# Rope and nope rows of an attention group loaded whole, after the group before it in the same place

## The reference, cut to what matters

```
q  = (ql @ Wqu)  -> 16 heads x 16 features      ("nope" part of the query)
qr = rope(ql @ Wqr) -> 16 heads x 64 features   (rotary part of the query)
k  = (ckv @ Wku) -> 16 heads x 16 features      (nope part of the key)
kr = rope(x @ Wkr)  -> 64 features, one for all heads
scores = (q k^T + qr kr^T) / sqrt(80), causal mask, softmax over s
out = softmax(scores) v
```

## Time and profile before

| | |
|---|---|
| median of 3 runs | 1025.59 us (1021.88 to 1035.82) |
| the profiled execution | 1023.33 us, span 1021.5 us |
| TensorE (PE) busy | 881.4 us, 86% of the span |
| VectorE (DVE) busy | 565.9 us, 55% |
| ScalarE (ACT) busy | 381.5 us, 37% |
| GpSimd (POOL) busy | 228.1 us, 22% |
| mean granted TensorE clock | 0.901 of full |
| bytes moved by DMA | 69.96 MB, 68 GB/s over the span |

### The profile page before, as it was taken

One profiled execution on the slowest core, in us unless ns is written; L12 is line 12 of the kernel. 1 busy time (PEld: TensorE's weight loads), 2 busy tenths in 40 slices (PEclk: granted clock), 3 DMA queues, 4 the chain that ended last, 5 costly groups with the idle time before them and its releaser, 6 DMA issues.

```text
span 1021.5 us, 11944 instructions
## 1 busy us (share of the span) xinstructions
PE 881.4 (86%) x4799; PEld 509.0 (50%) x4799; DVE 565.9 (55%) x988; ACT 381.5 (37%) x470; POOL 228.1 (22%) x209
## 2 busy tenths in 40 slices
PE   3988598999899986898698998978999879969897
PEld 3443244344335432453346878543333248868676
DVE  4697264767476544651533355377777335954452
ACT  2312043444444433446334340213555664410331
POOL 2451032233112303411310100220111126710010
PEclk9987598899799967999787999876999989989799
DMA  5389416521922292001300000494400042000001
GB/s 169 83 214 176 115 42 132 96 63 50 175 46 51 82 172 84 2 14 57 137 9 1 1 0 19 143 173 69 58 2 1 1 185 73 1 1 1 1 1 42
DMA packets 37936, 69.96 MB, mean 68 GB/s; under 512 B 6085, under 2 KB 14829, under 8 KB 37877
## 3 DMA queue, kind: packets, MB, share of 16 engines
q1 hardware_dynamic: 37880, 69.20, 29.1%
HBM read 49.07 MB, written 18.38 MB: 66 GB/s over the span
## 4 chain that ended last, share of the span: by engine, by line
PE 59%; DVE 17%; DMA 9%; ACT 5%; SPq 5%; POOL 3%; issue 2%; DVEq 0%; ACTq 0%; POOLq 0%
PE psD L1572 10%; PE psO L1693 9%; PE psA L1572 9%; PE psD L1638 8%; DVE mx L1180 7%; PE psO L1572 7%; PE psA L1656 7%; SPq L471 5%; PE psA L1655 3%; DVE hid_low L1486 2%; PE psD L1640 2%; DMA d_gq<-Pr 1%; PE psA L1604 1%; DMA Qs<-mrowb 1%; ACT Pr L908 1%
## 5 line engine op out<-in xcount | busy, mean ns | idle before, releaser
L1180 DVE TENSOR_REDUCE mx<-psD 128x1 f32<-128x512 f32 (+3 forms) x417 | 260.9, 658 | 143.1 <-PE psD L1640 101.9
L908 ACT ACTIVATE Pr<-psA 128x1024 f32<-128x1024 f32 (+3 forms) x192 | 162.3, 865 | 226.2 <-PE psA L1656 225.5
L779 POOL TENSOR_SCALAR_AFFINE_SELECT Pr<-Pr 128x512 f32<-128x512 f32 x96 | 60.9, 635 | 432.9 <-ACT Pr L908 360.6
L1655 PE MATMUL psA<-Qr,Kr 128*128 128x512 f32 (+3 forms) x192 | 76.7, 413 | 11.6 <-DMA Qr<-mrow 11.6
L913 ACT ACTIVATE Pr<-psA 128x1024 f32<-128x1024 f32 (+3 forms) x96 | 63.4, 702 | 54.3 <-PE psA L1656 53.8
L1693 PE MATMUL psO<-Pr,Vh 128*32 128x512 f32 (+3 forms) x768 | 80.9, 501 | 2.9 <-POOL Pr L779 2.2
L1640 PE MATMUL psD<-maskq,identb 128*128 128x128 bf16 x348 | 75.8, 241 | 0.0
L1656 PE MATMUL psA<-Qr,Kr 113*128 113x512 f32 (+3 forms) x192 | 66.7, 354 | 0.0
L1656 PE MATMUL psA<-Qs,Kg 97*128 97x512 bf16 (+3 forms) x192 | 53.9, 380 | 14.6 <-DMA Qs<-mrowb 12.1
L1638 PE MATMUL psD<-Kr,Qr 80*128 80x512 bf16 (+3 forms) x166 | 62.6, 416 | 3.5 <-DVE mx L1180 2.9
L1638 PE MATMUL psD<-Kg,Qs 96*128 96x512 bf16 (+3 forms) x192 | 57.3, 339 | 5.0 <-POOL Pr L779 2.0
(11 more groups left out here) (409 smaller groups left out, 1680.6 us busy)
## 6 DMA issues: line engine op xcount, KB each, us to landing
Qr<-d_qr SPq DMA_DIRECT2D x24, 512.0 KB, 11.0
d_qr<-WB SPq DMA_DIRECT2D x9, 512.0 KB, 2.6
Pr<-d_cb SPq DMA_DIRECT2D x8, 512.0 KB, 7.0
Qr<-d_qn SPq DMA_DIRECT2D x24, 128.0 KB, 7.9
Kr<-d_kn SPq DMA_DIRECT2D x24, 128.0 KB, 8.9
Qs<-d_gq SPq DMA_DIRECT2D x24, 128.0 KB, 4.6
Qs<-d_q SPq DMA_DIRECT2D x24, 128.0 KB
Ks<-d_k SPq DMA_DIRECT2D x24, 128.0 KB
```

Of the source, the lines that this page charges most:

```text
L779: pool.affine_select(out=block_, in_=block_, pattern=[[0, GH], [1, P]], compare_op=ALU.is_ge, fill=0.0, base=0, channel_multiplier=-1).the ...
L908: act.activation(place[:, h, q0:T], src[:, q0:T], ACT.Exp, scale=score_scale(i)).then_inc(a_drained, 1)
L1180: dve.tensor_reduce(mx[:, j, part, h0:h0 + nh], src, AX, ALU.max).then_inc(d_drained, 1)
L1655: pe.matmul(out_, second[0], second[1](lo, (half + 1) * HALF), start=True, stop=False)
```

## The change

`load_high` and `load_rest` take no half any more: each of their DMAs moves all 1024 columns of each head. The early `load_high(i + 2, 0)` and its wait for tile 3 are gone; the whole of `load_high(i + 2)` is issued behind `maxima_row(i + 1)` and the wait for all scores of group i, with `load_rest(i + 2)` right behind it. The pairs of semaphores become one each, and the wait in the middle of the maxima goes.

```diff
-            def load_mla(i, half, places, s):
-
-                c = slice(half * HALF, (half + 1) * HALF)
+            def load_mla(i, places, s):
+
                 for t, a, n, d in places:
                     g = head_group(i) * GH * n
-                    load(t[a:a + n, 0:GH * T].bitcast(F32).rearrange("p (h t) -> p h t", h=GH)[:, :, c],
-                         d[g:g + GH * n, :].rearrange("(h d) t -> d h t", d=n)[:, :, c], s[half])
+                    load(t[a:a + n, 0:GH * T].bitcast(F32).rearrange("p (h t) -> p h t", h=GH),
+                         d[g:g + GH * n, :].rearrange("(h d) t -> d h t", d=n), s)
...
             sp.wait_ge(nope_stored, 16 * 2)
-            load_high(0, 0)
-            load_high(0, 1)
+            load_high(0)
...
-            load_rest(0, 0)
-            load_rest(0, 1)
+            load_rest(0)
...
                     sp.wait_ge(rope_stored, 16 * 2 * (i + 4))
                     sp.wait_ge(nope_stored, 16 * 8)
-                    sp.wait_ge(a_filled, scored(i, NT // 2 - 1))
-                    load_high(i + 2, 0)
                 if i + 1 in GROUPS[0]:
                     maxima_row(i + 1)
                 if is_mla(i) and i < 2 * NG - 2:
                     sp.wait_ge(a_filled, A[f"att{i}"])
-                    load_high(i + 2, 1)
-                    load_rest(i + 2, 0)
-                    load_rest(i + 2, 1)
+                    load_high(i + 2)
+                    load_rest(i + 2)
...
             def maxima_unit(i, j, h0, nh, w, part):
 
-                if is_mla(i) and (j, h0, part) == (NT // 2, 0, 0):
-                    pe.wait_ge(mla_in[1], 16 * MLA_DMAS * (i // 2 + 1))
...
                 if is_mla(i):
-                    pe.wait_ge(mla_in[0], 16 * MLA_DMAS * (i // 2 + 1))
+                    pe.wait_ge(mla_in, 16 * MLA_DMAS * (i // 2 + 1))
                     pe.wait_ge(kr_in, 16 * N_KR)
...
-                        for half in range(2):
-                            pe.wait_ge(rest_in[half], 16 * REST_DMAS * (i // 2 + 1))
+                        pe.wait_ge(rest_in, 16 * REST_DMAS * (i // 2 + 1))
```

More of the change, by code:

```diff
@@ L445, in build @@
         split_stored = [sem(f"split_stored{n}") for n in range(3)]
-        mla_in, rest_in = ([sem(f"{s}{n}") for n in range(2)] for s in ("mla_in", "rest_in"))
+        mla_in, rest_in = sem("mla_in"), sem("rest_in")
         shared_in = [sem(f"shared_in{n}") for n in range(2)]
@@ L500, in rope_store, with load_high, load_rest @@
                 load(d_qr[part, tile_cols(p), :], rope_place(p)[1 - part], rope_stored)
-            def load_mla(i, half, places, s):
-                c = slice(half * HALF, (half + 1) * HALF)
+            def load_mla(i, places, s):
                 for t, a, n, d in places:
                     g = head_group(i) * GH * n
-                    load(t[a:a + n, 0:GH * T].bitcast(F32).rearrange("p (h t) -> p h t", h=GH)[:, :, c],
-                         d[g:g + GH * n, :].rearrange("(h d) t -> d h t", d=n)[:, :, c], s[half])
-            def load_high(i, half):
-                load_mla(i, half, ((Qr, 0, RD, d_qr[0]), (Qr, RD, HD, d_qn[0]), (Kr, RD, HD, d_kn[0])), mla_in)
-            def load_rest(i, half):
-                load_mla(i, half, ((Qr, RD + HD, HD, d_qn[0]), (Qr, RD + 2 * HD, HD, d_qn[1]),
-                                   (Kr, RD + HD, HD, d_kn[1]), (Kr, RD + 2 * HD, HD, d_kn[0]),
-                                   (Qr2, 0, RD, d_qr[0]), (Qr2, RD, RD, d_qr[1])), rest_in)
+                    load(t[a:a + n, 0:GH * T].bitcast(F32).rearrange("p (h t) -> p h t", h=GH),
+                         d[g:g + GH * n, :].rearrange("(h d) t -> d h t", d=n), s)
+            def load_high(i):
+                load_mla(i, ((Qr, 0, RD, d_qr[0]), (Qr, RD, HD, d_qn[0]), (Kr, RD, HD, d_kn[0])), mla_in)
+            def load_rest(i):
+                load_mla(i, ((Qr, RD + HD, HD, d_qn[0]), (Qr, RD + 2 * HD, HD, d_qn[1]),
+                             (Kr, RD + HD, HD, d_kn[1]), (Kr, RD + 2 * HD, HD, d_kn[0]),
+                             (Qr2, 0, RD, d_qr[0]), (Qr2, RD, RD, d_qr[1])), rest_in)
             def load_stack(i):
```

## The result

| | before | after |
|---|---|---|
| median of the runs | 1023.73 us (1021.83 to 1035.82, 4 runs) | 1051.45 us (1048.85 to 1054.02, 4 runs) |
| the profiled execution's span | 1021.5 us | 1049.5 us |
| mean granted TensorE clock | 0.901 | 0.886 |

The changed kernel takes 27.7 us longer: ratio 1.0245, 95% interval 1.0161 to 1.033. The predicted time was 1042, the range 1031 to 1052; the time lies 0.6 us under its upper end.

A forecast was written before the change was run, and what follows sets the result against it. TensorE was taken to set the time, with DMA mattering where TensorE stands still for it. Three transitions, 6.7 + 7.6 + 3.7 = 18.0 us, on 1023.3 gave 1041.3, called 1042 against the median; range 1031 to 1052.

The forecast's parts named there:

- The row of maxima: At the first transition mrowb leaves near 164.3, ahead of the high rows; TensorE's 4.62 us wait for it goes.
- The high rows' issue: At the transitions the whole high rows are issued when the group's scores are done: 167.71, 262.90 and 357.60.
- The landing: Whole high rows land 12.7 us after issue, ending each transition; first maxima units start 6.7, 7.6 and 7.6 us later.
- The give-back: Behind the third transition, TensorE's wait near 392 for GpSimd and W_up shrinks, so that transition costs +3.7, not 7.6.
- The start: At the kernel's start, whole loads cost 0: TensorE's wait for VectorE until 72.77 hides a delay under 1 us.
- The clock: At the transitions, longer waits add no half-clock time; full clock returns some 15 us after the first maxima unit. Cost nothing.
- The sum: Over the whole kernel: 6.7 + 7.6 + 3.7 = 18.0 us slower.
- case D: Third transition not given back, or clock low a stretch more: +22 to +30, 1045 to 1054 us; chance 0.14.
- the main case: The prediction's own case for the whole kernel: late whole high rows cost +14 to +22 us; chance 0.68.
- B: Part of a DMA's cost is per transfer, so whole high rows take 10.9 us; sum about 8, 1032 us; chance 0.13.
- C: No loss or a gain: whole load lands at the 9.8 us bound; sum +1, 1025 us; chance 0.05.

The follow-up runs named there:

- the crossing of the weights' place: The weights' four loads moved ahead of group 6's rest, in the kernel before (1015.3 us) and in the changed kernel (1041.81 us).

## Why the prediction came out as it did

**The row of maxima.** As said: issued at 166.20 in front of the high rows (predicted near 164.3; in this execution all stands 1.9 us later from group 0 on), and its wait gone.

**The high rows' issue.** As said, at the end of the group's scores: 169.71, less the 1.93 by which group 0's scores started later, is 167.78 against the predicted 167.71.

**The landing: the term that was mis-sized.** The prediction took 12.7 us for the whole, as the sum of two halves, because "a whole load from an idle queue moves the bytes of both with nothing between". For two halves behind each other that was right (12.9 measured), and for whole rows alone on the queue too (12.7 on average). The whole rows with the rest behind them took 14.3, 13.4 and 13.6 us. The single DMAs of the first transition show where (issue size, us from issue to landing; issued at 169.71, 170.39 and 171.05):

```profile
Qr<-d_qr SPq DMA_DIRECT2D x1, 1024.0 KB, 9.3
...
Qr<-d_qn SPq DMA_DIRECT2D x1, 256.0 KB, 11.0
Kr<-d_kn SPq DMA_DIRECT2D x1, 256.0 KB, 12.9
```

The 64 rope rows take 9.3 us (8.8 and 8.6 at the other two), not the 7.6 of the earlier trace rows, which the prediction had as a lower bound. The two sets of 16 rows land 4.9 us behind them (184.0 less 179.0). The flow while 64-row loads move, in the kernel after:

```profile
171.50:176.50 5.00, 0.00 (x0) 0.00 (x0) 0.00 (x0) 0.41 (x1) 0.00 (x0) 0.86 0.98 218
```

and in the kernel whose rest is issued only behind the high rows, where nothing else is on the queue: the 64-row load, the two 16-row sets, and the last 2.3 us before TensorE goes on at 179.75:

```profile
170.00:174.50 4.50, 0.00 (x0) 0.00 (x0) 0.00 (x0) 0.00 (x0) 0.00 (x0) 0.72 1.06 228
174.50:177.00 2.50, 0.00 (x0) 0.00 (x0) 0.00 (x0) 0.00 (x0) 0.00 (x0) 0.50 1.05 110
...
177.50:179.80 2.30, 0.05 (x1) 0.05 (x2) 0.00 (x0) 0.00 (x0) 0.00 (x0) 0.50 0.06 7
```

The rates are no slower than the prediction's 221 and 133, which it read off single microseconds, except that the 133 is 110 where nothing but 16-row sets moves. What it had no term for is the end of the load: with nothing behind, the flow has all but stopped at 177.5, 10.2 us after the first issue, and the last rows count as landed only near 179.7. With the rest behind, the 14.30, 13.40 and 13.60 us of the three transitions moved 2.04, 1.94 and 2.00 MB (length times GB/s in the table above), while the high rows are 1.57 MB (1536 KB): 0.37 to 0.47 MB of the rest had moved before the last of them was in. (In halves, both awaited, it was 0.3 to 0.4 MB.) That fits the 1.0 us by which the rest lengthens the landing on average. Which DMA engine lands last, and why, no run here shows.

The Trainium skill, page "SBUF — State Buffer", section "Door 1: The DMA port swizzle", has about 218 GB/s as the limit for 64 partitions and 109 for 16; by it and about 2 us fixed the whole was estimated at 11.6 us. The trace agrees with both rates (218 to 228 and 110) and not with the sum: 12.3 to 13.5 us alone, 13.1 to 14.3 with the rest behind.

As first-maxima times, +6.7, +7.6 and +7.6 became +8.3, +8.3 and +8.4: 3.1 us in all.

**The give-back.** 3.9 predicted, 3.9 measured by the stretches, 4.0 by the crossing of the weights' place. The wait near 392 fell to 4.73 ("about 4"). Its size held although the landing did not, since W_up follows the high rows on the same queue: its issue came 16.3 us behind the first maxima unit before (379.09 less 362.75) and 12.5 after (402.58 less 390.04), and it took 11.3 and 11.1 us to land.

**The start.** Costed at 0; 2.1 in this pair of profiles, 0.8 on average over all fourteen, within their scatter.

**The clock.** The step said that a longer wait costs no further time at half clock behind it. It held at the transitions: it comes back 15.0 us after the first maxima unit (184.0 to 199.0), where the prediction said some 15; at the other two transitions it takes 14.6 and 14.0, against 13.8, 15.0 and 15.8 in the kernel before. These two stages of the kernel after are the last at half and the first at full clock:

```profile
198.00:199.00 1.00, 1.00 (x7) 0.43 (x4) 0.24 (x1) 0.00 (x0) 0.00 (x0) 0.51 0.80 160
199.00:200.00 1.00, 1.00 (x11) 0.47 (x8) 0.90 (x2) 0.67 (x1) 0.00 (x0) 1.00 0.22 49
```

But half clock elsewhere took its share, which the prediction had no term for. The second profile of the very same changed kernel has two stretches that the first lacks, in groups 2 and 4. The first (from:to, length, busy times, then PEclk as the third number from the right):

```profile
247.50:255.50 8.00, 7.89 (x27) 2.80 (x28) 3.33 (x6) 0.81 (x1) 0.00 (x0) 0.57 0.00 0
255.50:263.00 7.50, 7.29 (x50) 3.83 (x48) 4.67 (x8) 2.85 (x4) 2.97 (x2) 1.00 0.01 2
```

and the same place in the first profile of the changed kernel:

```profile
247.00:257.00 10.00, 8.87 (x43) 3.73 (x41) 7.86 (x13) 2.76 (x4) 1.28 (x1) 1.00 0.23 92
```

They cost 3.5 and 4.2 us: from first maxima to next high issue it takes 93.0 and 93.7 us with them, 89.5 without. From the first high issue to the end of layer 0's attention the changed kernel took 425.4 us in one profile and 430.9 in the other; the kernel before 401.1 and 400.7. So the loss in this part was 24.3 and 30.2, and the medians' 27.7 and, measured again, 29.4 lie between. Of the fourteen places (groups 2 and 4, seven profiles each) ten have such a stretch in kernels with late high rows and four in those with early ones. That suggests that late rows bring them on, some 3 us on average, but the same kernel has none or two, so it is not shown.

**The sum.** Predicted +18.0. Measured without such stretches: 25.0 at the transitions, -3.9 given back, 0.3 + 0.8 in the groups and 2.1 at the start, 24.3. The 3.1 of the landing and the 2.1 of the start make 5.2 of the 6.3 between them. The other 3.4 of the 27.7 are not placed by these profiles: in this pair the remainder lies behind layer 0's attention (+3.9), in the second pair in the stretches at half clock (3.5 and 4.2). The mechanism was the one forecast, and its size was that of case D (+22 to +30), to which the prediction gave 0.14, though not by D's mechanisms: W_up landed 23.6 us behind the third first maxima unit, as said (23.8), and the clock did not stay low longer after the waits. Only D's remark that clock stretches vary between places bore on it. That the time fell inside the range is partly luck: the same kernel measured again has a median of 1054.27, outside it, and the main case of +14 to +22, which had 0.68, missed both.

**The rivals.** B falls by the direct comparison (12.9 in halves, 13.7 whole). The Trainium skill, page "DMA: Bandwidth & Descriptors", section "Rules for kernel authors", tells one to join many small transfers into a large one, those under 64 KB above all; with 128 to 512 KB each already, joining two gained nothing here. C needed a landing under 6 us and falls with it.

## What to carry to other kernels

Early loads into a place that is free in part are worth the time that their bytes take, not the length of the wait one sees in the profile: here a 4.6 us wait for a small row hid that the half ahead of it on the queue needed 7.9. Before splitting or joining loads, ask what the consumer's first unit needs. Halves let it start after half of the bytes, and that was worth about as much here (12.6 us of kernel time) as the early issue (14.0). And the one gain over the kernel before, 9.6 us, lay in neither: it was the order on the queue of two loads of which one was wanted early and the other late.

## What the runs showed of the hardware

- A load of 64, 16 and 16 partitions, 1.5 MB in all, took 13.7 us in runs of 4 KB and 12.9 in runs of 2 KB, both with 3 MB queued behind. The load in runs of 4 KB took 12.7 with nothing behind. All are means; the values with and without the 3 MB overlap (13.1 to 14.3, and 12.3 to 13.5).
- On one queue, 64-row loads moved at 218 to 228 GB/s and 16-row loads at 110. With nothing behind, the last 2.3 us of the load moved at 7 GB/s.
- SP's issue of a small load lasted 19.0 us in the kernel after (`su`, at 382.79) and 11.6 in the kernel before, each with the 3 MB of the rest and the 1 MB of W_down queued ahead of it, and 0.58 us where only high rows and W_down were ahead. What SP had to issue next waited as long.
- Two executions of the same kernel can differ by whole stretches of 7 to 10 us at half clock inside dense work, each worth some 3.5 to 4 us. Longer runs of a kernel tend to be those with the lower mean granted clock (1020.22 us at 0.904, 1030.51 at 0.890, both of the kernel before), so such stretches may be much of the scatter of 1 to 2% among runs; that is not shown.
